# Attention projections from high and low float32r parts, value masking in one step, batches written out

## The reference, cut to what matters

```
src_trans = (einsum('bsf,of->bso', src, W_src) + b_src) * src_mask   # keys and values, 512 -> 512
tgt_trans = (einsum('btf,of->bto', tgt, W_tgt) + b_tgt) * tgt_mask   # queries, 256 -> 256
scores = q k^T / sqrt(32), -inf where src_mask == 0; attn = softmax(scores)
tgt_update = attn v                                                  # 256 features
out = einsum('btf,of->bto', concat(tgt, tgt_update), W_out) + b_out  # 512 -> 256
x = x + tanh(gate) * out
```

## Time and profile before

| what | value |
|---|---|
| median of three runs | 690.71 us |
| the profiled execution, device time | 689.92 us |
| its span in the profile | 687.1 us |
| PE busy (matmul) | 644.9 us, 94%, 3490 matmuls |
| PEld busy (weight load) | 440.5 us, 64% |
| DVE busy | 430.2 us, 63% |
| ACT busy | 434.3 us, 63% |
| POOL busy | 202.5 us, 29% |
| DMA queue of the data | 57.33 MB, 30.4% of 16 engines |
| DMA queues of the instructions (q8, q14) | 22 packets, 0.36 MB, and 24 packets, 0.20 MB |
| granted TensorE clock | 0.99 of full, mean over the span |
| chain that ended last | PE 75%, SP's queue 8%, DMA 4%, DVE 4%, ACT 3% |

### The profile page before, as it was taken

The page is one execution under the profiler, slowest core; times in us unless marked ns, Lnnn a source line. Parts: engine busy times, 40 slices in busy tenths (PEclk is TensorE's granted clock), DMA queues, the critical chain, the costliest instruction groups (busy, mean ns, idle before and its releaser), DMA issues.

```text
span 687.1 us, 11443 instructions
## 1 busy us (share of the span) xinstructions
PE 644.9 (94%) x3490; PEld 440.5 (64%) x3490; DVE 430.2 (63%) x982; ACT 434.3 (63%) x1164; POOL 202.5 (29%) x299
## 2 busy tenths in 40 slices
PE   4988899999999998699999999999999987899997
PEld 2764555555544457588877878888888865656654
DVE  7974758786775748376666666666666686152522
ACT  7666655535544433577777778777787777545452
POOL 6575423310110012124443333333332220142110
PEclk9999999999999999899999999999999999899999
DMA  8821116401000005534434544444444440001112
GB/s 283 258 78 62 60 33 245 96 1 62 0 1 0 1 0 126 127 78 110 107 89 118 125 115 105 107 109 107 100 103 124 93 94 3 1 14 50 53 40 92
DMA packets 43124, 57.88 MB, mean 84 GB/s; under 512 B 6118, under 2 KB 25926, under 8 KB 42950
## 3 DMA queue, kind: packets, MB, share of 16 engines
q1 hardware_dynamic: 43078, 57.33, 30.4%
HBM read 27.46 MB, written 4.19 MB: 46 GB/s over the span
## 4 chain that ended last, share of the span: by engine, by line
PE 75%; SPq 8%; DMA 4%; DVE 4%; ACT 3%; issue 3%; POOL 2%; DVEq 0%; POOLq 0%; ACTq 0%
PE bank L1134 12%; SPq L504 7%; PE bank L1420 6%; PE bank L1146 6%; PE bank L1331 6%; PE bank L1350 6%; PE bank L1396 4%; PE bank L1556 4%; PE bank L1373 4%; PE bank L1359 4%; PE bank L1110 3%; PE bank L1413 3%; PE bank L1546 3%; DMA c_stack<-neg_row 2%; PE bank L1114 2%
## 5 line engine op out<-in xcount | busy, mean ns | idle before, releaser
L931 ACT ACTIVATE c_junk<-bank,c_nmx 128x256 bf16<-128x256 f32 x256 | 117.5, 486 | 15.7 <-DVE c_nmx L1883 15.5
L1883 DVE TENSOR_REDUCE c_nmx<-bank 128x4 f32<-128x1024 f32 x64 | 75.4, 1219 | 36.9 <-PE bank L1373 36.9
L1134 PE MATMUL bank<-b_o,cw 128*128 128x512 f32 x192 | 90.6, 603 | 1.8 <-ACT b_o L795 1.8
L953 ACT ACTIVATE c_pT<-bank 128x1024 f32<-128x1024 f32 x64 | 61.7, 1014 | 5.9 <-PE bank L1396 5.6
L771 ACT ACTIVATE b_h<-bank,cols 128x512 f32<-128x512 f32 x48 | 32.9, 687 | 51.0 <-PE bank L1134 50.8
L1042 ACT ACTIVATE d_h<-bank,cols 128x512 f32<-128x512 f32 x64 | 39.7, 686 | 39.3 <-PE bank L1547 39.3
L1134 PEld LDWEIGHTS bank<-b_o,cw 128*128 128x128 f32 x192 | 34.5, 190 | 44.9 <-issue 41.1
L1331 PE MATMUL bank<-c_ctxT,wsrcT 128*128 128x256 f32 x256 | 61.8, 386 | 0.4 <-DVE c_vb L1875 0.4
L1350 PE MATMUL bank<-wsrcT,c_ctxT 128*128 128x256 f32 x240 | 56.7, 379 | 0.0
L1396 PE MATMUL bank<-c_stack 99*128 99x256 f32 x256 | 48.4, 322 | 8.6 <-DMA c_stack<-c_rows 8.2
L931 ACT ACTIVATION_READ_ACCUMULATOR c_junk<-bank,c_nmx 128x1 f32 x256 | 55.8, 218 | 0.0
(11 more groups left out here) (184 smaller groups left out, 1298.3 us busy)
## 6 DMA issues: line engine op xcount, KB each, us to landing
c_stack<-c_parts SPq DMA_DIRECT2D x192, 128.0 KB
a_ctx<-in_ctx SPq DMA_DIRECT2D x16, 512.0 KB, 3.9
c_ctxT<-in_ctx_turned SPq DMA_DIRECT2D x16, 512.0 KB, 3.6
out_x<-x_sb SPq DMA_DIRECT2D x7, 512.0 KB, 2.9
x_sb<-in_x SPq DMA_DIRECT2D x3, 1024.0 KB, 9.5
mask_b<-in_mask SPq DMA_DIRECT2D x1, 2048.0 KB, 11.9
x_sb<-in_x SPq DMA_DIRECT2D x2, 512.0 KB, 5.6
wsrcT<-in_w_src_turned SPq DMA_DIRECT2D x1, 1024.0 KB, 7.0
```

What stands on the lines that cost most here:

```text
L931: op = nc.scalar.activation(c_junk[:, tc, j, :], scores(tc)[:, j, :], ACT.Exp, bias=c_nmx[hg][:, tc, j:j + 1], accum_out=c_sum[hg][:, tc, ...
L953: nc.scalar.activation(c_pT[hg][:, :, q * S:(q + 1) * S], scores(q), ACT.Exp).then_inc(c_pT_ok, 1)
L1134: op = mm(bank[2 * u + h][:], cw1[:, c, h * P:(h + 1) * P], b_o[n % LANES][:, c, :], start=c == 0, stop=c == DK - 1)
L1883: v.tensor_reduce(c_nmx[hg][:, tc, :], scores(tc), AXIS.X, ALU.max, negate=True)\
```

## The change

1. The three weight matrices and the four moving or stationary operands (context, normalised x, update) are kept as a high float32r part and a low one (the rest, also float32r). Each projection matmul in float32 becomes three in float32r (`product`): high x high, high x low, low x high.
2. The parts: POOL splits the weights once (`split_weights`) and the context of each batch (`split_x`, one copy and one subtraction over 1024 columns). ACT writes the high part of normalised x (`xn_hi`) and of the update (the old copies, now with a float32r output), DVE the low ones from PSUM (`xn_lo`, 512 columns, `up_lo`, 256 columns twice a batch). ACT's second copy `c_xnT` goes, with three generations of `c_nhi` and `c_nlo` in its place.
3. Values: POOL makes `c_bvm`, bias times mask (`masked_bias`, two steps of 256 columns), and DVE writes `c_v` from PSUM in one kind of step, times mask plus `c_bvm` (two instructions). `c_vb` and ACT's two steps go.
4. All batches are written out on all engines; addresses are constants.
5. Memory moves: `c_xn` and the landing place `c_x` of the context have one buffer each. The attention weights land in memory of part A and are loaded once that part is done, `v1` in batch 1.

The places in the order are in the diff (cut; renamed semaphores and the memory plan are left out).

```diff
-def over_batches(eng, body):
-    for b in range(HEAD):
-        body(b, b % 2)
-    with eng.Fori(HEAD // 2, B // 2 - 1) as i:
-        body(2 * i, 0)
-        body(2 * i + 1, 1)
-    for b in range(B - 2, B):
+def over_batches(body):
+    for b in range(B):
         body(b, b % 2)
...
# SP
             weights_in(loads_d, s_wd)
             sp.wait_ge(a_out_ps, B)
+            weights_in(loads_w, s_ww)
+            weights_in(loads_c, s_wc)
...
-            def stream_c(b, s):
-                need(sp, c_v_ps, b - 1)
-                sp.dma_start(c_ctxT[s][:], ctxT_dram[b]).then_inc(c_ctx_in[s], 16)
+            def stream_c(b):
+                need(sp, c_x_ok, b)
+                sp.dma_start(c_x[:], ctxT_dram[b]).then_inc(c_ctx_in, 16)
...
-                if b + 3 < B:
-                    stream_c(b + 3, 1 - b % 2)
+                if b + 4 < B:
+                    stream_c(b + 4)
+                if b == 1:
+                    sp.wait_ge(b_x2, NG)
+                    weights_in(loads_v1, s_v1_in)
...
# POOL
+            def split_weights():
+                pool.wait_ge(s_ww, 16 * len(loads_w))
+                nc.gpsimd.tensor_scalar(wtgt_raw[:], wtgt_raw[:], SCALE, None, ALU.mult).then_inc(s_wscaled, 1)
+                nc.gpsimd.tensor_copy(wsrc_hi[:], wsrc_raw[:]).then_inc(s_whi, 1)
...
+            def split_x(b):
+                pool.wait_ge(c_ctx_in, 16 * (b + 1))
+                need(pool, c_v_ps, b - 1)
+                nc.gpsimd.tensor_copy(c_xhi[b % 2][:], c_x[:]).then_inc(c_xhi_ok, 1)
+                pool.wait_ge(c_xhi_ok, b + 1)
+                nc.gpsimd.tensor_tensor(c_xlo[b % 2][:], c_x[:], c_xhi[b % 2][:].bitcast(F32), ALU.subtract)\
+                    .then_inc(c_x_ok, 1)
+            def masked_bias(b):
+                need(pool, c_v_ok, b)
+                for k in range(TS):
+                    op = nc.gpsimd.tensor_scalar(c_bvm[:, k, :], bv_b[:], mask_col[:, b, k:k + 1], None, ALU.mult)
+                op.then_inc(c_bvm_ok, 1)
...
                 if not is_last(b, B):
                     split_q(b + 1)
                     bias_c(b + 1)
+                if not beyond(b + 3, B):
+                    split_x(b + 3)
+                if not beyond(b + 2, B):
+                    masked_bias(b + 2)
...
+            split_x(0)
+            split_x(1)
+            pool.wait_ge(s_wc, 16 * len(loads_c))
+            masked_bias(0)
             split_q(0)
             split_k(0)
-            pool.wait_ge(s_scaled, 6)
+            pool.wait_ge(s_scaled, 5)
             bias_c(0)
             split_k(1)
+            split_x(2)
+            masked_bias(1)
...
# ACT, body_c
                     update_c(b - 1, 1 - s, 1)
-                v_c(b + 1, 1 - s)
                 rows_c(b, 0)
...
                 probsT_c(b, 0, 1)
-                xnT_c(b + 1, 1 - s)
                 if ahead:
-                    xnTq_c(b + 2)
+                    xn_hi(b + 2)
                 update_c(b, s, 0)
...
# PE
+            def product(dst, left, right, first, last):
+                mm(dst, left[0], right[0], start=first, stop=False)
+                mm(dst, left[0], right[1], start=False, stop=False)
+                return mm(dst, left[1], right[0], start=False, stop=last)
...
-                    op = mm(bank[4][:, k * D:(k + 1) * D], c_ctxT[s][:, f, k * P:(k + 1) * P],
-                            wsrcT[:, f, D:2 * D], start=f == 0, stop=f == FK - 1)
+                    op = product(bank[dst][:, k * D:(k + 1) * D], (c_xhi[s][:, f, at], c_xlo[s][:, f, at]),
+                                 (wsrc_hi[:, f, D:2 * D], wsrc_lo[:, f, D:2 * D]), f == 0, f == FK - 1)
...
# DVE
+            def xn_lo(b, src=5):
+                need(dve, c_nhi_ok, b + 1)
+                v.tensor_tensor(c_nlo[b % GENS][:].rearrange("p c t -> p (c t)"), bank[src][:],
+                                c_nhi[b % GENS][:].rearrange("p c t -> p (c t)").bitcast(F32), ALU.subtract)\
+                    .then_inc(c_nlo_ok, 1)
+            def up_lo(b, s, hg):
+                need(dve, c_uphi_ok, 2 * b + hg + 1)
+                v.tensor_tensor(c_uplo[s][:, hg, :], bank[6][:, hg * S:(hg + 1) * S],
+                                c_uphi[s][:, hg, :].bitcast(F32), ALU.subtract).then_inc(c_up_ok, 1)
...
-            def v_c(b, src=4):
+            def v_c(b, s, src=4):
                 need(dve, c_v_ps, b + 1)
-                need(dve, c_v_ok, b)
-                v.tensor_tensor(c_vb[:], bank[src][:].rearrange("p (k d) -> p k d", k=TS),
-                                bv_b[:].unsqueeze(1).to_broadcast([P, TS, D]), ALU.add).then_inc(c_vraw, 1)
+                need(dve, c_bvm_ok, b + 1)
+                need(dve, c_up_ps, 2 * (b - 1))
+                for k in range(TS):
+                    op = v.scalar_tensor_tensor(c_v[s][:, k, :], bank[src][:, k * D:(k + 1) * D],
+                                                mask_col[:, b, k:k + 1], c_bvm[:, k, :], ALU.mult, ALU.add)
+                op.then_inc(c_v_ok, 1)
...
                 shift_c(b, 0)
-                v_c(b + 1)
+                v_c(b + 1, 1 - s)
+                if not first:
+                    up_lo(b - 1, 1 - s, 1)
                 maxima_c(b, s, 1)
...
                     biased(c_kT, bank[4], bk_col, b + 2, c_k_ps, c_k_ok, c_k_split, 2 * (b + 2))
+                    xn_lo(b + 2)
+                up_lo(b, s, 0)
...
-            xn_c(0, 0)
-            xn_c(1, 1)
+            xn_c(0)
             slot_b(PAIRS - 2)
+            xn_lo(0, 6)
...
             slot_b(PAIRS)
+            xn_c(1)
             x_b(NG - 2)
             biased(c_kT, bank[4], bk_col, 1, c_k_ps, c_k_ok, c_k_split, 2)
-            over_batches(dve, body_c)
+            xn_lo(1)
+            over_batches(body_c)
             xn_d(2)
+            up_lo(B - 1, 1, 1)
             finish_c(B - 1, 1)
```

More of the change, by code:

```diff
@@ L60 @@
 SCALE = 1.0 / math.sqrt(HD)
+GENS = 3
 PARTS = 4
@@ L313, in build @@
         with ExitStack() as st:
-            sb("c_first", [P, 4 * KB + KB // 2], F32, st)
+            sb("raw_first", [P, 78 * KB // 4], F32, st)
+            wsrc_raw = sb("wsrc_raw", [P, FK, 2 * D], F32, st)
+            wtgt_raw = sb("wtgt_raw", [P, DK, D], F32, st)
+            wout_raw = sb("wout_raw", [P, 2 * DK, D], F32, st)
+        with ExitStack() as st:
+            sb("c_first", [P, 18 * KB // 4], F32, st)
+            c_pT = [sb(f"c_pT{h}", [P, QH, TS * S], F32, st) for h in range(2)]
+            c_uphi = [sb(f"c_uphi{s}", [P, DK, S], F32R, st) for s in range(2)]
             c_junk = sb("c_junk", [P, TS, QH, S], BF16, st)
@@ L322, in build @@
             c_rows = [sb(f"c_rows{h}", [TS * SHIFTS * QH, P], F32R, st) for h in range(2)]
-            sb("c_second", [P, 2448 + S], F32, st)
-            c_pT = [sb(f"c_pT{h}", [P, QH, TS * S], F32, st) for h in range(2)]
-            c_xnT = [sb(f"c_xnT{s}", [P, DK, S], F32, st) for s in range(2)]
-            c_upT = [sb(f"c_upT{s}", [P, DK, S], F32, st) for s in range(2)]
+        with ExitStack() as st:
+            sb("c_second", [P, 44 * KB // 4], F32, st)
+            c_nhi = [sb(f"c_nhi{g}", [P, DK, S], F32R, st) for g in range(GENS)]
+            c_nlo = [sb(f"c_nlo{g}", [P, DK, S], F32R, st) for g in range(GENS)]
+            c_xn = sb("c_xn", [P, TS, D], F32, st)
+            c_kT = sb("c_kT", [P, DK, S], F32, st)
+            c_uplo = [sb("c_uplo0", [P, DK, S], F32R, st)]
             c_stack = [None, sb("c_stack1", [MASK_ROW + 1 + SHIFTS, 2, QH, DK, S], F32R, st)]
             c_stack[0] = sb("c_stack0", [MASK_ROW + 1 + SHIFTS, 2, QH, DK, S], F32R, st)
-            sb("c_third", [P, 8 * KB // 4], F32, st)
-            c_ctxT = [sb(f"c_ctxT{s}", [P, FK, S], F32, st) for s in range(2)]
-            c_xn = [sb(f"c_xn{s}", [P, TS, D], F32, st) for s in range(2)]
-            c_xnTq = sb("c_xnTq", [P, DK, S], F32, st)
-            c_kT = sb("c_kT", [P, DK, S], F32, st)
+            c_xhi, c_xlo = [None] * 2, [None] * 2
+            for s in range(2):
+                c_xhi[s] = sb(f"c_xhi{s}", [P, FK, S], F32R, st)
+                c_xlo[s] = sb(f"c_xlo{s}", [P, FK, S], F32R, st)
+            c_x = sb("c_x", [P, FK, S], F32, st)
             c_qT = sb("c_qT", [P, DK, S], F32, st)
@@ L339, in build @@
             c_v = [sb(f"c_v{s}", [P, TS, D], F32, st) for s in range(2)]
-            c_vb = sb("c_vb", [P, TS, D], F32, st)
+            c_bvm = sb("c_bvm", [P, TS, D], F32, st)
+            c_uplo.append(sb("c_uplo1", [P, DK, S], F32R, st))
+            mask_b = sb("mask_b", [P, B, S], F32, st)
+        with ExitStack() as st:
+            sb("v1_first", [P, 8 * KB // 4], F32, st)
+            v1_sb = sb("v1_sb", [P, F // P, P], F32, st)
         with ExitStack() as st:
@@ L430, in build @@
         ]
+        loads_v1 = [(v1_sb[half * RANK:(half + 1) * RANK], v1.rearrange("r (c f) -> r c f", f=P)) for half in range(2)]
         loads_d = [
             (u1_sb[:], u1.rearrange("(c p) r -> p c r", p=P)),
```

(22 more changed lines are left out.)

160 lines of the change are left out of this document (83 added, 77 removed).

## The result

The changed kernel takes 702.08 us (median of 4 executions, 700.10 to 703.05); the kernel before, run beside it, 690.28. The ratio is 1.018, with a 95% interval of 1.0143 to 1.0217: slower by 1.8%. The forecast of 693.0 us was 9 us short. The time lies in the range of 684 to 706, but the likeliest outcome, no change within 1%, did not come. That it lies in the range is luck: the bounds of the range were made from other terms, and some 8 us of the loss come from Pool's work in part B, which was put at nothing.

What follows compares the result with a forecast made beforehand. The prediction took two coinciding bounds in part C, PE and a circle through DVE and ACT; the profiled 689.92 us plus 1.3 for the beat and 1.8 for part C's start gave 693.0 us, range 684 to 706.

Steps and rivals of the forecast that it cites:

- The cheaper product: Part C projections on PE: a float32r matmul takes 0.12 us, three 0.36 against 0.433, saving 2.0 us of work a batch.
- the circle: Chain in half A through DVE maxima, ACT sums and exponentials, and PE's update, filling 9.45 us by itself without any projection.
- rival 1: Part C: PE's saving comes through, 28 us less in full (665) or 7 less in a modest form; chance 0.13.
- The sign named: Evidence if right: PE's idle time before half A's update grows from nothing to about 1 us, under ACT's `c_pT`.
- Half A: First half of a part C batch, scores to scores: 9.45 us plus 0.15 for maxima delayed by `up_lo`, giving 9.60.
- Half B: Second half of a part C batch, up to the next batch's scores: 9.75 us forecast against 9.81 before.
- The beat: Time from one batch's scores to the next in part C: 19.35 us against 19.26, +1.3 us over 14 batches.
- Weight splitting: Some 13 us of POOL in part B, costed at nothing because POOL is idle and readers come 60 us later.
- rival 3: Part C: POOL's `split_x` holds up DVE's shift chain in each batch, +18 us, 711 in all; chance 0.09.
- The start of part C: POOL reaches `split_q(1)` 2.4 us late behind `split_x(2)` and `masked_bias(1)`; with a saving on keys and queries, +1.8 us.
- The 0.9 us for cheaper keys and queries: Start of part C: batch 0's keys and queries, 12 matmuls saving 0.073 us each, come 0.9 us earlier.
- Rival 2: Part C: written-out code makes the mask row land late in every batch, +15 us, 708 in all; chance 0.20.

Runs made afterwards that it cites:

- Experiment 4: The changed kernel with the two products of low parts left out of every projection: 713.35 us, ratio 1.0315 to the kernel before.
- experiment 5: The changed kernel with a third buffer for the masked values, so VectorE's values step waits for updates one batch older: 701.07 us.
- experiment 2: The changed kernel with weights split by VectorE where it waits, and Pool's first two context splits held until part B's last update chains: 694.43 us, ratio 1.0051.
- experiment 3: The kernel before with Pool's seven operations on the weights added, their results read by nobody: 695.94 us, ratio 1.0085.
- Experiment 8: The kernel of experiment 2 with the third context's split and second masked bias moved on Pool behind the loop's first query split: 694.10 us, ratio 1.0057.
- experiment 7: The changed kernel with the v1 split cut into eight pieces, one in each of batches 5 to 12: 699.24 us, ratio 1.0126 to the kernel before.
- experiment 9: The changed kernel with the next batch's mask row issued ahead of the last four stack copies on SP's queue: 704.26 us, ratio 1.0219.

## Why the prediction fell short, by its own steps

- **The cheaper product: right.** 0.12 us a matmul was forecast, 0.11 to 0.12 measured.
- **PE's saving hidden by the circle: right,** and rival 1 is out: the beat stayed at 19.2 us with PE idle in 14.3 of 150 us. Experiment 4 took another two thirds of the projections away and no time with them, though at a lower clock. The place of the idle time was wrong. The sign named was about 1 us ahead of the update of half A; in batch 10 PE has 0.09 us there, and 0.39 and 0.67 ahead of turned scores and 0.38 ahead of the turning of the shift rows.
- **Half A, forecast 9.60, measured 9.25.** The sign of this term was wrong. `up_lo` was to delay the maxima by 0.15 us; it ends before they could start. Of the rest, 0.07 is the loop (9.45 in it, 9.38 in straight code), and 0.13 probably the circle no longer meeting PE's work.
- **Half B, forecast 9.75, measured 9.97.** The failed step is "DVE's `v_c` becomes two steps [...] done before the update of half A has ended". It starts after it: the step took over ScalarE's wait for the updates of the batch before, and everything behind it on VectorE waits too. The delay of the maxima is 0.46 us, at the upper bound of 0.45, for another reason than the one given. Behind it the sum had no term for SP's queue, which binds half B as tightly in batches 5, 9 and 10 of the changed kernel and in all short ones of experiment 5; the prediction had named it only as a way to fail.
- **The beat, forecast 19.35, measured 19.2.** Two misses of opposite sign. Where +1.3 us was forecast, the steady beat costs nothing.
- **Weight splitting "lies in part B, where POOL is idle; its readers come 60 us later": the step that failed.** Pool's own time was forecast as 13 us and measured as 14.3, so the size was right. But it was costed at nothing because nobody waits for it. Its price is what it does to VectorE while it runs. Together with the first context splits it cost 7.85 us in the profile and 6.8 to 7.7 in timed runs (experiment 2); the weights alone, in the kernel before, 5.1 and 6.6 (experiment 3). The earlier trace rows showed the mechanism, a 1.01 us step beside a 1.28 us addition, and rival 3 named it, but only for the shift steps of part C. There the subtraction of `split_x` meets one in batch 6 alone (2.34 us), and its copy in batch 6 and once in batch 0 (0.94 us). It was never laid against the VectorE rows beside the new work in part B.
- **The start of part C, forecast +1.8, measured +2.4: right in the main.** POOL comes to the query parts 10.9 us later than before, 2.4 beyond part B's delay, which is the forecast's own figure, though `masked_bias` takes 1.84 us and not 0.8 (bounds 0.6 to 1.3). The 0.9 us for cheaper keys and queries was lost to the low clock. Experiment 8 shows that SP's queue has the same wait in it, which the prediction had passed over when it called the load of a context one issue behind the mask row.
- **The v1 split** wasn't in the sum, since it doesn't change. But its 3.4 us of Pool now meet a queue that is three quarters fuller (90.07 against 51.60 us in the same window): about 2 to 2.8 us (experiment 7).
- **Rival 2, mask rows late in all batches written out: half right.** They land late in five batches of the changed kernel, 4, 8, 9, 12 and 14, the same five both times it was profiled, and hold up four of these (9 was in time all the same); the kernel before has seven (3 to 8 and 15), and written out it has eleven. In its loop none is late from batch 9 on. On the time of the kernel before this has no effect that can be measured, but it eats what the third buffer gains.

## What to carry to other kernels

Work on Pool with no reader nearby is not free: list the VectorE instructions that run beside it and ask whether they are on the chain. Here only steps with their operands in SBUF were stretched. When a step moves to another engine, its waits move too, and everything behind it on that queue now waits for them. Before a saving on the busiest engine is counted, take that engine's work away altogether and see whether the beat moves, and read the granted clock beside it. When one wait goes, look in the chain for the next one: here it was the order on SP's queue, 0.47 us behind.

## What the runs showed of the hardware that was not expected

- A Pool subtraction of 2048 columns (4.53 us) held a VectorE step of 256 columns, 0.33 us a piece otherwise, until its end. VectorE came through once or twice between two of Pool's instructions, so Pool's length counts, not VectorE's. It goes both ways: `c_bvm`, 1.84 us alone, took 2.77 beside part B's recurrence. This is the exclusive lock of "SBUF — State Buffer", section "SBUF: two separate sides", in the Trainium skill, which the prediction had cited; the trace agrees, in part B as in part C. VectorE steps that read a PSUM bank were never stretched, in the whole changed kernel: the 64 maxima took 1.207 to 1.226 us each, the 32 steps of `v_c` 0.470 to 0.489 and the 32 of `up_lo` 0.411 to 0.425, while `c_xlo` ran from 491.01 to 493.40 beside three of them in the batch above.
- Leaving two thirds of the projection matmuls out made the changed kernel 11 to 12 us slower, through the granted clock (0.83 instead of 0.99).
- The last transfers of a batch on SP's queue land up to 2 us late (the row 3.75 us after its issue, against 2.02 in the other batches) in certain batches. They are the same ones in both profiled executions of the changed kernel and in both of the kernel with the third buffer (4, 8, 9, 12 and 14), and it is whichever transfer is last (4.42 us for a copy in experiment 9). What makes it late stays open. Writing the kernel before out raised the number from seven batches to eleven, but the changed kernel, also written out, has five. A fetch of code isn't shown either: the page counts 22, 28 and 32 packets on an instruction queue (q8) for these three, which doesn't go with seven, eleven and five.
